# Two late projections behind the first turns, first rows and first row of maxima on two queues, three banks for folded differences

## The reference

```
q, k, v = x Wq' + bq, x Wk' + bk, x Wv' + bv          # 16 heads of 8
attn    = softmax(q k' / 4) v                         # per head, 1024 x 1024
x1      = layernorm(x + attn Wo' + bo)
h       = silu(x1 W1' s1) * (x1 W2' s2)               # 512 wide
h       = gelu(h H1' t1);  h = gelu(h H2' t2)
out     = layernorm(x1 + h W3' s3)
```

## Time and profile before

| | us |
|---|---|
| Median of three runs | 448.09 |
| The profiled execution | 446.64 |
| Its span, first to last instruction | 444.8 |
| TensorE busy | 429.2 (96%) |
| VectorE busy | 385.5 (87%) |
| ScalarE busy | 368.1 (83%) |
| GpSimd busy | 90.5 (20%) |
| TensorE clock granted, mean | 0.995 |

### The profile page before, as it was taken

One profiled execution on the slowest core, in us unless ns is written; L12 is line 12 of the kernel. 1 busy time (PEld: TensorE's weight loads), 2 busy tenths in 40 slices (PEclk: granted clock), 3 DMA queues, 4 the chain that ended last, 5 costly groups with the idle time before them and its releaser, 6 DMA issues.

```text
span 444.8 us, 9805 instructions
## 1 busy us (share of the span) xinstructions
PE 429.2 (96%) x3484; PEld 225.6 (51%) x3486; DVE 385.5 (87%) x724; ACT 368.1 (83%) x696; POOL 90.5 (20%) x142
## 2 busy tenths in 40 slices
PE   8999999999999999999999999999899899999993
PEld 3544444444444444444444443545343488877882
DVE  5589999999999999999999999999739477657636
ACT  4477888989998899998899899999889976678762
POOL 9810000100000010000001002372310262046103
PEclk9999999999999999999999999999999999999997
DMA  5665840110130111013011111121021000000101
GB/s 148 181 204 104 291 146 28 49 28 27 49 122 25 34 42 28 27 47 122 25 42 36 25 27 49 15 41 55 9 39 48 13 8 1 1 3 1 47 1 47
DMA packets 16988, 24.88 MB, mean 56 GB/s; under 512 B 5040, under 2 KB 8880, under 8 KB 16560
## 3 DMA queue, kind: packets, MB, share of 16 engines
q1 hardware_dynamic: 16304, 23.62, 19.1%
q10 hardware_dynamic: 640, 0.66, 0.6%
HBM read 15.08 MB, written 7.60 MB: 51 GB/s over the span
## 4 chain that ended last, share of the span: by engine, by line
PE 77%; DVE 12%; ACT 7%; issue 2%; POOL 0%; POOLq 0%; DVEq 0%; ACTq 0%
PE ps L1306 24%; PE ps L1228 21%; PE ps L1402 15%; DVE negmax L940 9%; PE ps L1290 9%; ACT arena L634 4%; PE ps L1170 2%; PE ps L1181 2%; DVE arena L930 1%; PE ps L1247 1%; PE ps L1352 1%; PE ps L1201 1%; PE ps L1256 1%; ACT v_pad L692 1%; ACT arena L647 1%
## 5 line engine op out<-in xcount | busy, mean ns | idle before, releaser
L940 DVE TENSOR_REDUCE negmax<-ps 128x1 f32<-128x512 f32 x458 | 275.3, 683 | 0.4 <-PE ps L1228 0.4
L634 ACT ACTIVATE arena<-ps 128x512 f32<-128x512 f32 x360 | 189.5, 611 | 19.9 <-PE ps L1290 15.1
L1290 PE MATMUL ps<-qx,kx 64*128 64x512 f32 x512 | 172.7, 453 | 1.2 <-DVE negmax L940 0.9
L1228 PE MATMUL ps<-kx,qx 61*128 61x512 f32 x464 | 160.1, 444 | 0.8 <-ACT arena L655 0.6
L1228 PEld LDWEIGHTS ps<-kx,qx 61*128 61x128 f32 x464 | 74.4, 184 | 91.2 <-DVE negmax L940 83.5
L1306 PE MATMUL ps<-arena,v_pad 128*32 128x256 f32 (+3 forms) x1328 | 104.6, 407 | 3.1 <-ACT arena L634 3.0
L634 ACT ACTIVATE hf<-ps 128x512 f32<-128x512 f32 x152 | 83.1, 603 | 8.2 <-PE ps L1290 7.0
L1290 PEld LDWEIGHTS ps<-qx,kx 64*128 64x128 f32 x512 | 80.0, 184 | 14.0 <-ACT arena L634 7.4
L1402 PE MATMUL ps<-hid,w_high 128*128 128x512 f32 (+1 forms) x296 | 68.2, 387 | 0.8 <-issue 0.4
L1402 PEld LDWEIGHTS ps<-hid,w_high 128*128 128x128 f32 x296 | 54.2, 188 | 12.4 <-issue 0.8
L1306 PEld LDWEIGHTS ps<-arena,v_pad 128*32 128x32 f32 x1328 | 28.4, 108 | 39.2 <-issue 31.2
(11 more groups left out here) (96 smaller groups left out, 322.6 us busy)
## 6 DMA issues: line engine op xcount, KB each, us to landing
qx<-parts_q SPq DMA_DIRECT2D x60, 64.0 KB, 2.1
late_sb<-in_late SPq DMA_DIRECT2D x3, 1280.0 KB, 5.6
kx<-parts_k SPq DMA_DIRECT2D x48, 64.0 KB, 2.1
parts_q<-prt SPq DMA_DIRECT2D x3, 512.0 KB, 5.2
parts_q<-arena SPq DMA_DIRECT2D x3, 512.0 KB, 5.7
xT_sb<-in_xT SPq DMA_DIRECT2D x4, 256.0 KB, 4.0
kx<-parts_k SPq DMA_DIRECT2D x8, 128.0 KB, 3.3
xT_sb<-arena SPq DMA_DIRECT2D x28, 32.0 KB
```

Source lines behind the costliest of these rows:

```text
L634: nc.scalar.activation(probs(n // HG)[:, heads(n), :], ps[:, PLAN["score", n][0], :], ACT.Exp, scale=SCALE).then_inc(exp_done, 1)
L940: nc.vector.tensor_reduce(negmax[:, t // TURNS % 2, m % 2, h * QT + q:h * QT + q + 1], ps[:, MAX_BANK + m % 4, :], AX.X, ALU.max, negate=T ...
L1228: nc.tensor.matmul(ps[:, MAX_BANK + m % 4, :], qx[at, slot, qc, h, q * P:(q + 1) * P], kx[at, slot, h, part * C:(part + 1) * C], start=Tru ...
L1290: nc.tensor.matmul(ps[:, bank, :], kx[at, slot, h % PAIR, kt * P:(kt + 1) * P], qx[at, slot, qc, h % PAIR, :], start=True, stop=True)\
```

## The change

All edits lie in the first 40 us.

1. FOLD goes from 3 to 5: five plain turns, then 22 folded ones (11 pairs in place of 12). Their banks are given by `half_bank` and the waits of `fold_first` are rewritten for it.
2. Of the four late projections two stay ahead of the turns; the other two are issued behind turns 1 and 2. The two filler matmuls ahead of the first turn, those between plain turns, and those behind the pairs from turn 21 on are gone (only the pair that starts with turn 25 has some, behind a wait for `copy_max`). The filler writes to bank 7.
3. The rows of the first unit are loaded by two queues: two of the four `qx` loads stay on ScalarE's queue, two go to SP's. The two stores of the key difference go from SP's queue to ScalarE's.
4. The difference matmuls use three banks (6, 1, 0) in place of two.
5. The first row of maxima: `larger(0, 0)` is left out (the second column of `negmax` holds 3e38 there), GpSimd reads `negmax` itself. The transpose stands behind the pair of turns 21 and 22 (before: 19 and 20), ScalarE's copy of it behind its copy for turn 22 (before: 20). Of the two DMAs of this row one is issued by ScalarE right behind its copy, the other by SP.

```diff
@@ -68,2 +68,3 @@
-FOLD = 3
-FOLD_BANKS = (6, 1)
+FOLD = 5
+TURN_AFTER, COPY_AFTER = 5, 6
+FOLD_BANKS = (6, 1, 0)
@@ -187 +188 @@
-WARM, FILL = 9, 2
+WARM, FILL_BANK, AHEAD_JOBS = 9, 7, 6
@@ -201,0 +203,8 @@
+def apart_bank(t):
+    return FOLD_BANKS[(t - FOLD) % len(FOLD_BANKS)]
+def half_bank(m):
+    return MAX_BANK + (m + 2 * (FOLD // 2 + 1) if m < 2 * FOLD else m) % 4
@@ -383,0 +393,8 @@
+        def spread_max(queue, r, w):
+            slot, qc = w // QC % 2, w % QC
+            queue.dma_start(qx[r * GROUP + TROWS:r * GROUP + MROWS, slot, qc].bitcast(F32)
+                            .rearrange("i h t -> i (h t)"),
+                            mT[PARTS * TURNS // 2 * r:PARTS * TURNS // 2 * (r + 1), w % 2, :])\
+                 .then_inc(mrow_in[w % 2], 16)
@@ -431,3 +448 @@
-            def load_max(i, w):
-                slot, qc = w // QC % 2, w % QC
+            def load_max(i, w, rs=(0, 1)):
@@ -436,5 +451,2 @@
-                for r in range(2):
-                    sp.dma_start(qx[r * GROUP + TROWS:r * GROUP + MROWS, slot, qc].bitcast(F32)
-                                 .rearrange("i h t -> i (h t)"),
-                                 mT[PARTS * TURNS // 2 * r:PARTS * TURNS // 2 * (r + 1), w % 2, :])\
-                      .then_inc(mrow_in[w % 2], 16)
+                for r in rs:
+                    spread_max(sp, r, w)
@@ -448,6 +460,6 @@
-            sp.wait_ge(apart_high, 1)
-            sp.dma_start(d_dram[:, :, 0].rearrange("h d t -> (h d) t"), kd_part[0][0:HG * DH, :])\
-              .then_inc(apart_out, 16)
-            sp.wait_ge(apart_low, 1)
-            sp.dma_start(d_dram[:, :, 1].rearrange("h d t -> (h d) t"), kd_part[1][0:HG * DH, :])\
-              .then_inc(apart_out, 16)
+            sp.wait_ge(q_first, STORE_INC)
+            for i in range(HALVES):
+                at = GROUP + i * HALVES * DH
+                sp.dma_start(qx[at:at + HALVES * DH, 0, 0].bitcast(F32),
+                             q_dram[i, 0, 0, PAIR:2 * PAIR].rearrange("h d j t -> (d j) h t"))\
+                  .then_inc(rows_in[0][0], 16)
@@ -471 +483 @@
-            load_max(0, 0)
+            load_max(0, 0, (0,))
@@ -617,6 +629,11 @@
-            for r in range(2):
-                for i in range(HALVES):
-                    at = r * GROUP + i * HALVES * DH
-                    act.dma_start(qx[at:at + HALVES * DH, 0, 0].bitcast(F32),
-                                  q_dram[i, 0, 0, r * PAIR:(r + 1) * PAIR].rearrange("h d j t -> (d j) h t"))\
-                       .then_inc(rows_in[0][0], 16)
+            for i in range(HALVES):
+                at = i * HALVES * DH
+                act.dma_start(qx[at:at + HALVES * DH, 0, 0].bitcast(F32),
+                              q_dram[i, 0, 0, 0:PAIR].rearrange("h d j t -> (d j) h t"))\
+                   .then_inc(rows_in[0][0], 16)
+            act.wait_ge(apart_high, 1)
+            act.dma_start(d_dram[:, :, 0].rearrange("h d t -> (h d) t"), kd_part[0][0:HG * DH, :])\
+               .then_inc(apart_out, 16)
+            act.wait_ge(apart_low, 1)
+            act.dma_start(d_dram[:, :, 1].rearrange("h d t -> (h d) t"), kd_part[1][0:HG * DH, :])\
+               .then_inc(apart_out, 16)
@@ -655 +672 @@
-                nc.scalar.activation(over_sb(t), ps[:, FOLD_BANKS[t % 2], :], ACT.Relu).then_inc(over, 1)
+                nc.scalar.activation(over_sb(t), ps[:, apart_bank(t), :], ACT.Relu).then_inc(over, 1)
@@ -659 +676 @@
-                if t == TURNS + 4:
+                if t == TURNS + COPY_AFTER:
@@ -660,0 +678,2 @@
+                    act.wait_ge(max_copied, 1)
+                    spread_max(act, 1, 0)
@@ -786 +805,4 @@
-                m, rest = (t.rearrange("p (r n) -> p r n", r=2) for t in (negmin[:, w % 2, :], mrest[:]))
+                first = i is None
+                i = 0 if first else i
+                m, rest = (t.rearrange("p (r n) -> p r n", r=2)
+                           for t in (negmax[:, 0, 0, :] if first else negmin[:, w % 2, :], mrest[:]))
@@ -792 +814,4 @@
-                pool.wait_ge(max_ready, i * PER + w + 1)
+                if first:
+                    pool.wait_ge(max_taken, 2 * TURNS)
+                else:
+                    pool.wait_ge(max_ready, i * PER + w)
@@ -815 +840 @@
-            split_max(0, 0)
+            split_max(None, 0)
@@ -920 +945 @@
-                bank = MAX_BANK + 2 * (t % 2)
+                bank = half_bank(2 * t)
@@ -959,3 +984,2 @@
-                if t == TURNS - 1:
-                    dve.wait_ge(max_preset, 1)
-                    larger(0, 0)
+            dve.wait_ge(max_preset, 1)
+            dve.wait_ge(max_split, 1)
@@ -1205 +1229 @@
-            for n in range(EARLY, len(JOBS)):
+            for n in range(EARLY, AHEAD_JOBS):
@@ -1207,2 +1230,0 @@
-            pe.wait_ge(proj_ready, 1)
-            busy(FILL, FIRST_BANKS[1])
@@ -1228 +1250 @@
-                nc.tensor.matmul(ps[:, MAX_BANK + m % 4, :],
+                nc.tensor.matmul(ps[:, half_bank(m), :],
@@ -1243 +1265 @@
-                pe.wait_ge(max_taken, 2 * (t - 3) if t >= FOLD + 4 else 2 * (FOLD - (fold_bank(t) - MAX_BANK) // 2))
+                pe.wait_ge(max_taken, 2 * (t - 3) if t >= FOLD + 4 else 2 * (FOLD - 1 + (t - FOLD) // 2))
@@ -1253 +1275 @@
-                if t >= FOLD + 2:
+                if t >= FOLD + len(FOLD_BANKS):
@@ -1255,2 +1277,2 @@
-                    pe.wait_ge(over, t - 1 - FOLD)
-                nc.tensor.matmul(ps[:, FOLD_BANKS[t % 2], :], rows, kd[at, h, :], start=True, stop=True)\
+                    pe.wait_ge(over, t - FOLD - len(FOLD_BANKS) + 1)
+                nc.tensor.matmul(ps[:, apart_bank(t), :], rows, kd[at, h, :], start=True, stop=True)\
@@ -1319,2 +1341,2 @@
-                busy(1, FIRST_BANKS[1])
-                busy(1, FIRST_BANKS[1], C // 2)
+                if 1 <= t <= len(JOBS) - AHEAD_JOBS:
+                    job(AHEAD_JOBS - 1 + t)
@@ -1329,3 +1351,4 @@
-                busy(1, FIRST_BANKS[1])
-                busy(1, FIRST_BANKS[1], C // 2)
-                if t == TURNS + 3:
+                if t < TURNS + TURN_AFTER:
+                    busy(1, FILL_BANK)
+                    busy(1, FILL_BANK, C // 2)
+                if t == TURNS + TURN_AFTER:
@@ -1334,0 +1358,4 @@
+                if t > TURNS + TURN_AFTER + 2:
+                    pe.wait_ge(max_copied, 1)
+                    busy(1, FILL_BANK)
+                    busy(1, FILL_BANK, C // 2)
```

## The result

The changed kernel takes 452.79 us (median of four runs, 452.57 to 453.06). The kernel before takes 447.75 on the same chip (four runs, 446.45 to 448.43). The ratio is 1.0123, 95% interval 1.0101 to 1.0145: 1.2% slower, outside the range that was given. The profiled execution took 452.57 us, its span is 450.8, and the mean granted clock of TensorE is 0.972 in place of 0.995.

What follows compares the result with a forecast made beforehand. VectorE's reductions pace the kernel, so only the main loop's start at 40.49 us counts: -1.35 + 0.9 + 0.35 - 0.77 + 0.65 - 0.1 = -0.3 us, giving 447.8 us, range 445.6 to 449.6.

Steps and rivals of the forecast that it cites:

- TensorE's clock holds: Whole kernel: the forecast's sum of -0.3 us took TensorE at full clock, 2.4 GHz; no term for a fall.
- TensorE's clock falls: Rival, chance 0.13: half clock when the main loop starts costs 2.7 us, sum +2.4, time 450.5.
- between 20 and 39 us TensorE has room: Turns ahead of the main loop: a low clock there would not matter; only one after 40 us would.
- First rows, -1.35: Start of the turns: q rows on two queues land at 17.15, first reduction at 18.1 instead of 19.45; bounds -0.9, -1.6.
- the first rows gain nothing: Rival, chance 0.12: q row loads land at 17.6 as before, sum +0.15, time 448.2.
- Two more plain turns and the late projections, +0.9 and +0.35: Turns: two plain ones cost 1.13 instead of 0.69 us each; the projection behind turn 2 delays turn 3 by 0.35.
- `larger` gone, -0.77: VectorE behind turn 15: the next reduction follows after 0.61 us, at 32.32 instead of 33.09.
- the third bank, -0.1: Folded turns: a third difference bank gains 0.02 us in four turns, some 0.1 us over 22.
- The ring of four turns: Folded turns: the S1 banks alone hold four turns to 2.76 us, 0.69 each, though VectorE's own pace is 0.61.
- The DMA on ScalarE, +0.65: Copy of the maxima: issuing the DMA, 0.45 to 0.87 us, makes turn 23 0.9 late, 0.27 recovered; from +0.2 to +0.8.

Runs made afterwards that it cites:

- e1: Changed kernel plus ten filler matmuls behind the two early late projections, ahead of the first half: 450.36 us, ratio 1.0063 to the kernel before.
- e15: Changed kernel with two difference banks, front, folded-pair and last-plain-turn fillers, both maxima DMAs on SP, transpose placed as before: 448.12 us, 1.0026 of the kernel before.
- e5: Kernel before with only `larger(0, 0)` left out: 446.63 us, ratio 0.9989 to the kernel before.
- e6: Kernel before with a third bank for the folded differences, fillers moved to bank 7, the late ones behind the copy of the maxima: 447.19 us, ratio 1.0001.
- e3: Changed kernel plus ten fillers ahead of the first half and both DMAs of the first maxima row on SP: 449.45 us, ratio 1.0036 to the kernel before.
- e12: Kernel before without the fillers behind the pairs of turns 21, 23 and 25: 447.65 us, ratio 1.0014 to the kernel before.

## Why the prediction was wrong

**The step that failed: TensorE's clock holds.** The forecast's sum took a full clock as given. The rival "TensorE's clock falls" had the mechanism, one of the places (the stretch ahead of the main loop) and even the sentence "TensorE idles about 0.8 us more ahead of the first half"; but it had a chance of 0.13, and a price of 2.7 us for one fall. There were two falls. The first, which the rival did not price, cost 2.64 + 1.57 = 4.2 us (e1). The argument "between 20 and 39 us TensorE has room" was wrong: at half clock the two projections, 0.94 us each before, took 1.73 and 2.07 in front of halves that VectorE was waiting for.

The edit made that wait itself. The prediction counted what leaves the path (two projections and two fillers) and then found the rows late, at 17.25, where TensorE is free at 16.4. What it did not ask is what TensorE does in between. With its own numbers that is 17.25 - 16.4, the 0.8 us of the rival; with the rows at their usual time it is 2.32 us of nothing.

**First rows, -1.35.** Measured: nothing, outside the bounds of -0.9 and -1.6; even the rival "the first rows gain nothing" kept 0.9 of it. The split of the queues shows no gain, and 17.15 rested on the shortest landing seen. The first reduction is at 19.40. With fillers it is at 18.73 in e1 and 18.88 in e15, but there TensorE's work stands earlier from the start on: the first half comes 3.97 us behind the start of the first late projection in both (13.92 to 17.89, 14.07 to 18.04), as before (14.64 to 18.61), and 4.20 in the changed kernel (14.39 to 18.59).

**Two more plain turns and the late projections, +0.9 and +0.35.** Right, at full clock: turn 3 waits 0.35 in e1. By the prediction the first folded turn comes 3.98 + 2 x 1.13 + 0.35 = 6.59 us behind the first reduction. e1 has 6.69, e15 6.68.

**`larger` gone, -0.77, and the third bank, -0.1.** Measured -0.45 and -0.36 (e5, e6); the two errors cancel, which is luck. The prediction let the reduction behind `larger` follow at 0.61; it follows at 0.93, with a wait for the copy. The ring of four turns was right in that two waits lie side by side and the bank alone does not bring 0.61, but the bank gains 0.09 us in four turns, not 0.02. With five plain turns the sum is near: e3, with both, takes 14.59 for its 22 folded turns, by the prediction's terms without the DMA 17.06 - 2 x 0.69 - 0.77 - 0.1 = 14.81.

**The DMA on ScalarE, +0.65.** Measured 1.63 (e1 beside e3, in part at half clock). Its issue takes 1.35 us there; the bound of 0.87 came from the same DMA on SP.

With the clock held, e15 puts the main loop at 40.63, within 0.2 of the kernel before, and its profiled execution takes as long. It is not the changed kernel, though: it has two banks, both DMAs on SP and the earlier transpose, and its median is 0.26% above the kernel before. Nor would the sum have come out without the clock: by the split above the edits by themselves come to 0.19 + 1.63 = 1.8 us where -0.3 was forecast, since the first rows' -1.35 did not come and the DMA cost 1.0 more.

## What to carry to other kernels

Before taking work out of TensorE's stream, fillers above all, ask what it does in the time that is freed, not only what the path gains: here one wait of 2.32 us for a DMA, where projections and fillers had stood, cost 4.2 us through the clock, more than all edits together could gain. Ten fillers in it gave that back ahead of the loop; the median got 2.4 us, since another fall came 270 us later. So look for falls over the whole span, not only where the edit is. Where a forecast starts from the landing of a DMA, take it from several executions. One profiled execution shows what can happen; how often, only the mean clocks of the other runs tell. And where two edits together gain more than each alone, look where in the trace the gain lies before naming the reason.

## What the runs showed of the hardware

- The same work can go either way: between 314 and 320 us the kernel before has 2.08 and 2.31 of 3 us busy and kept 2.4 GHz in its profiled execution, e6 has 2.06 and 2.33 and fell to 1.2 GHz at 318.54. e1 has 1.41 of 3 in 317 to 320 and fell at 319.3, the changed kernel 1.40 in 322 to 325 and did not.
- A fall is not priced by its length alone. A fall of 6.8 us around the start of the main loop cost VectorE 0.5 us of the 44 reductions in e12 (from 39.0, loop at 40.4), 1.84 in e3 (from 40.6, loop at 40.7), 0.1 in e1 (from 39.4, loop at 41.6) and nothing in the changed kernel (from 43.5, loop at 46.5). Near 320 us a fall of 3.4 us cost 1.1 to 1.3 us of the span in five kernels, one of 6.8 us some 2.4 in e1.
- The issue of a DMA of three partitions from ScalarE took 1.35 us, that of the same on SP 0.94 at the same moment in the changed kernel, and 0.93 and 0.75 for the two in the kernel before; whether ScalarE's is longer when SP issues none is not shown. The issue of a q row load of 64 KB takes 0.43 to 0.46 on either.
- Four loads of 64 KB, issued in the same way, landed after 3.5 to 5.0 us (medians of nine kernels that issue them on one queue).
